# Moving two per-token normalisations of a graph layer from VectorE to ScalarE

## The reference, cut to what matters

```python
def _layernorm(x, axis=-1, eps=1e-05):
    m = jnp.mean(x, axis=axis, keepdims=True)
    v = jnp.var(x, axis=axis, keepdims=True)
    return (x - m) / jnp.sqrt(v + eps)
...
def _L1_gnn_ref(inp, adj, W1, W2, W3):
    h1, h2, h3 = inp @ W1, inp @ W2, inp @ W3          # einsums in the original
    e = leaky_relu(h1 @ h2^T, 0.2); e = where(adj > 0, e, -1e12)
    return relu(softmax(e) @ h3)

def _L1_ffn_ref(x, Wg, bg, W1, b1, W2, b2):
    gate_logits = xf @ Wg + bg
    top_w, top_i = top_k(gate_logits, 2)               # each token goes to 2 of 8 experts
    ...
x = x + _L1_gnn_ref(_layernorm(x), adj, ...)
x = x + _L1_ffn_ref(_layernorm(x), ...)
```

## Time and profile before

| what | us |
|---|---|
| median of 3 runs (lowest, highest) | 1738.74 (1738.03, 1741.6) |
| profiled execution, its own time | 1740.67 |
| its span in the trace | 1738.7 |
| DVE busy in the span | 1017.5 (59%) |
| PE busy in the span | 1287.0 (74%) |
| POOL busy in the span | 812.2 (47%) |
| ACT busy in the span | 740.3 (43%) |

### The profile page before, as it was taken

How to read it: one execution, slowest core, us unless ns; L and a number is a source line. 1 busy time by engine, 2 the same in 40 slices (tenths; PEclk the granted TensorE clock), 3 DMA queues, 4 the chain that set the end, 5 groups by cost and what they waited for, 6 DMA issues and landing times. The chain is left out here.

```text
span 1738.7 us, 34925 instructions
## 1 busy us (share of the span) xinstructions
PE 1287.0 (74%) x8909; PEld 1090.6 (63%) x8909; DVE 1017.5 (59%) x3818; ACT 740.3 (43%) x1710; POOL 812.2 (47%) x839
## 2 busy tenths in 40 slices
PE   3988888837677777349999995767773299999930
PEld 2777666726566667238888884545552189888920
DVE  1788888757767776335555553888885122222236
ACT  2555555515655555214444441443432155555510
POOL 3255555561455554614444443277676144445420
PEclk9999999968989988669999997888876599999975
DMA  6100000000000000145656563122211366766647
GB/s 157 23 1 0 0 0 0 1 1 1 20 28 28 25 25 27 40 133 190 201 189 199 191 201 105 55 71 73 71 36 41 104 214 219 218 217 220 218 133 203
DMA packets 134763, 168.57 MB, mean 97 GB/s; under 512 B 17584, under 2 KB 105520, under 8 KB 134704
## 3 DMA queue, kind: packets, MB, share of 16 engines
q1 hardware_dynamic: 98224, 122.49, 23.6%
q0 software_dynamic: 17408, 35.95, 5.9%
q10 hardware_dynamic: 19072, 9.46, 1.9%
HBM read 123.47 MB, written 44.37 MB: 97 GB/s over the span
## 5 line engine op out<-in xcount | busy, mean ns | idle before, releaser
L1602 POOL DMA_INDIRECT rows<-m_yb,m_dsti x288 | 276.6, 960 | 361.1 <-DVE m_dsti L1734 312.5
L1627 PE MATMUL psum<-m_xT,m_w 128*128 128x256 f32 (+1 forms) x864 | 200.2, 381 | 1.3 <-ACT m_xT L1668 1.3
L964 POOL DMA_INDIRECT dispatch<-a_flat,a1r_pos x128 | 129.9, 1015 | 111.4 <-DVE a1r_pos L945 69.4
L964 POOL DMA_INDIRECT dispatch<-g_flat,g1r_pos x128 | 133.2, 1041 | 74.3 <-DVE g1r_pos L945 37.3
L1627 PEld LDWEIGHTS psum<-m_xT,m_w 128*128 128x128 f32 (+1 forms) x864 | 149.1, 179 | 28.9 <-ACT m_xT L1668 1.9
L1701 DVE TENSOR_TENSOR m_yb<-psum,m_w 128x256 f32<-128x256 f32 x72 | 30.6, 425 | 218.6 <-PE psum L1642 218.6
L1683 ACT ACTIVATE m_sg<-psum,m_w 128x256 f32<-128x256 f32 x288 | 117.9, 471 | 92.4 <-PE psum L1632 91.3
L1632 PE MATMUL psum<-m_xT,m_w 128*128 128x256 f32 x576 | 141.2, 389 | 7.4 <-ACT m_xT L1666 7.4
L1642 PE MATMUL psum<-m_w,m_sg 128*128 128x128 f32 x1152 | 140.5, 275 | 0.6 <-DVE m_yb L1701 0.6
L1676 ACT ACTIVATE m_sg<-psum 128x256 f32<-128x256 f32 (+1 forms) x216 | 78.8, 382 | 142.9 <-PE psum L1627 98.5
L1717 DVE TENSOR_TENSOR m_hT<-psum,m_sg 128x256 f32<-128x256 f32 (+1 forms) x216 | 88.4, 422 | 83.7 <-ACT m_sg L1676 81.1
(11 more groups left out here) (250 smaller groups left out, 2971.2 us busy)
## 6 DMA issues: line engine op xcount, KB each, us to landing
m_w<-in_c_wall SPq DMA_DIRECT2D x72, 578.0 KB, 3.6
m_w<-in_c_wall SPq DMA_DIRECT2D x72, 533.0 KB, 3.4
m_xg<-dispatch SPq DMA_DIRECT2D x144, 130.0 KB, 3.5
g1c_y<-rows SPq DMA_DIRECT2D x32, 256.0 KB
fin_y<-rows ACTq DMA_DIRECT2D x32, 256.0 KB, 3.5
rows<-m_yb,m_dsti POOLq DMA_INDIRECT x288, 3.1
out<-x SPq DMA_DIRECT2D x16, 256.0 KB, 3.0
dispatch<-nobody SPq DMA_DIRECT2D x24, 130.0 KB, 6.8
```

The lines of the kernel that those rows point to most:

```text
L964: pool.indirect_dma_start(out=dest, out_offset=bass.IndirectOffsetOnAxis(ap=self.pos[:, k, p:p + 1], axis=0), in_=flat[:, p, :], in_offset ...
L1602: pool.indirect_dma_start(out=rows_out, out_offset=bass.IndirectOffsetOnAxis(ap=dsti[j][:, t:t + 1], axis=0), in_=yb[j][:, t, :], in_offse ...
L1627: i = pe.matmul(bank[0:cn, TILE * m:TILE * m + TILE], w[j][:, HID * m + c0:HID * m + c0 + cn], xT[j % 2][:, :], start=(m == 0), stop=True, ...
```

## The change

Both normalisations go to ACT, as `x * rs + off` with `off = -mean * rs` (an ACT instruction of the kind Identity, with `rs` as its scale and `off` as its bias, both read from SBUF). DVE forms `off` for the four tiles of a group in one instruction over 128 x 4. That instruction (`head_off`, `flat_off`) needs `rs`, and it stands in DVE's step behind `vector_choose` and ahead of `soft`. On ACT the second normalisation stands ahead of `exp`, the first one between `exp` and `probs_T`. POOL's order is the same, with one more wait in front of each `pow`.

```diff
@@ phase_gnn1
+        ve, rs, off = sb("ve", [128, 2, PG]), sb("rs", [128, 2, PG]), sb("off", [128, 2, PG])
...
             @block.scalar
+                def head_xn(i):
+                    act.wait_ge(*off_ready[0].now(i))
+                    act.wait_ge(*pe_xT.before(i))
+                    act.sem_inc(act_gate.sem, 1)
+                    for p in range(PG):
+                        act.activation(xn[:, p, :], xt(i, p), ACT.Identity, bias=off[:, 0, p:p + 1],
+                                       scale=rs[:, 0, p:p + 1]).then_inc(xn_ready.sem, 1)
+
+                def flat_norm(i, b):
+                    act.wait_ge(*off_ready[1].now(i))
+                    act.wait_ge(*pe_fT.before(i))
+                    R.wait_landed(act, i - 2)
+                    act.sem_inc(act_gate.sem, 1)
+                    for p in range(PG):
+                        act.activation(flat[b][:, p, 0:C], xt(i, p), ACT.Identity, bias=off[:, 1, p:p + 1],
+                                       scale=rs[:, 1, p:p + 1]).then_inc(flat_ready.sem, 1)
...
                 def step(g, b):
                     low(g)
                     head(g + 1)
+                    flat_norm(g - 1, 1 - b)
                     exp(g)
+                    head_xn(g + 2)
                     probs_T(g)
...
-                skewed(act, step)
+                skewed(act, step, first=4)
...
             @block.vector
-                def head_xn(i):
+                def head_off(i):
                     dve.wait_ge(*rs_ready[0].now(i))
-                    dve.wait_ge(*pe_xT.before(i))
-                    for p in range(PG):
-                        dve.tensor_scalar(xn[:, p, :], xt(i, p), mv[:, 0, p, 0:1], rs[:, 0, p:p + 1],
-                                          ALU.subtract, ALU.mult).then_inc(xn_ready.sem, 1)
+                    dve.wait_ge(*xn_ready.before(i))
+                    dve.scalar_tensor_tensor(out=off[:, 0, :], in0=mv[:, 0, :, 0], scalar=-1.0, in1=rs[:, 0, :],
+                                             op0=ALU.mult, op1=ALU.mult).then_inc(off_ready[0].sem, 1)
...
-                def flat_norm(i, b):
+                def flat_off(i):
                     dve.wait_ge(*rs_ready[1].now(i))
-                    dve.wait_ge(*pe_fT.before(i))
-                    R.wait_landed(dve, i - 2)
-                    for p in range(PG):
-                        dve.tensor_scalar(flat[b][:, p, 0:C], xt(i, p), mv[:, 1, p, 0:1], rs[:, 1, p:p + 1],
-                                          ALU.subtract, ALU.mult).then_inc(flat_ready.sem, 1)
+                    dve.wait_ge(*flat_ready.before(i))
+                    dve.scalar_tensor_tensor(out=off[:, 1, :], in0=mv[:, 1, :, 0], scalar=-1.0, in1=rs[:, 1, :],
+                                             op0=ALU.mult, op1=ALU.mult).then_inc(off_ready[1].sem, 1)
...
                 def step(g, b):
                     flat_stats(g - 1)
                     if runs(g - 2):
                         R.vector_choose(dve, g - 2, bR, False)
+                    head_off(g + 2)
+                    flat_off(g - 1)
                     soft(g)
                     if runs(g - 2):
                         R.vector_rows(dve, g - 2, bR)
-                    flat_norm(g - 1, 1 - b)
-                    head_xn(g + 2)
                     head_x(g + 3, 1 - b)
                     norm(g)
                     head_stats(g + 3)
...
             @block.gpsimd
                 def head_rs(i):
                     pool.wait_ge(*vs[0].now(i))
+                    pool.wait_ge(*off_ready[0].before(i))
                     pool.wait_ge(*xn_ready.before(i))
...
                 def flat_rs(i):
                     pool.wait_ge(*vs[1].now(i))
+                    pool.wait_ge(*off_ready[1].before(i))
                     pool.wait_ge(*flat_ready.before(i))
```

More of the change, by code:

```diff
@@ L1801, in phase_gnn1 @@
         st, mv = sb("st", [128, 2, PG, 6]), sb("mv", [128, 2, PG, 2])
-        ve, rs = sb("ve", [128, 2, PG]), sb("rs", [128, 2, PG])
+        ve, rs, off = sb("ve", [128, 2, PG]), sb("rs", [128, 2, PG]), sb("off", [128, 2, PG])
         xn = sb("xn", [128, PG, C])
@@ L1826, in phase_gnn1 @@
         flat_ready = sig("flat_ready", PG)
-        gate = sig("gate")
-        dve_signals = bn + part + vs + [xn_ready, e_steps, rc_ready, x3_ready, flat_ready]\
-            + R.dve_signals + M.dve_signals
+        off_ready = [sig("off0_ready"), sig("off1_ready")]
+        gate, act_gate = sig("gate"), sig("act_gate")
+        dve_signals = bn + part + vs + off_ready + [e_steps, rc_ready, x3_ready] + R.dve_signals + M.dve_signals
         xT_ready, h12_ready, p_ready, pt_ready, fT_ready = sig("xT_ready"), sig("h12_ready", 2), sig("p_ready", 2), sig("pt_ready"), sig("fT_ready")
         low_ready = sig("low_ready", 2)
-        act_signals = [xT_ready, h12_ready, h3_ready, low_ready, p_ready, pt_ready, o_ready, fT_ready] + R.act_signals
+        act_signals = [xn_ready, flat_ready, xT_ready, h12_ready, h3_ready, low_ready, p_ready, pt_ready, o_ready, fT_ready] + R.act_signals
         rs_ready = [sig("rs0_ready"), sig("rs1_ready")]
@@ L1963, in _ @@
             def _(act):
+                def head_xn(i):
+                    if not runs(i):
+                        return
+                    act.wait_ge(*off_ready[0].now(i))
[5 more added lines that the diff above has]
+                def flat_norm(i, b):
+                    if not runs(i):
+                        return
+                    act.wait_ge(*off_ready[1].now(i))
[5 more added lines that the diff above has]
+                                       scale=rs[:, 1, p:p + 1]).then_inc(flat_ready.sem, 1)
                 def head(i):
```

## The result

The changed kernel takes 1768.55 us in the median of 4 runs (1764.85 to 1769.39). The kernel before, on the same chip, takes 1740.17 us (1738.03 to 1743.23). The ratio is 1.0158, with a 95% interval from 1.0135 to 1.018: slower by 28 us. The forecast was 1761 us, in a range of 1752 to 1774.

What follows compares the result with a forecast made beforehand. DVE was taken to bound the loop before, a newly closed loop through POOL's `pow` after. Eleven periods +15.8, tail +5.2 and start +1.5 gave +22.5 us, a median of 1761 us, range 1752 to 1774.

Steps and rivals of the forecast that it cites:

- scatter to `pow`: Loop term on POOL, from a scatter's start to the next `pow`: 10.1 us, with ends 9.99 and 10.78.
- both `pow`: Loop term on POOL, the two `pow` behind a scatter: 2.05 us.
- offset, up to `soft`: Loop term on DVE, both new `off` instructions ahead of `soft`: 0.3 us, from 0.1 to 0.6.
- `soft` to scatter: Loop term from the start of `soft` on DVE to the scatter's start on POOL: 4.31 us, low end 4.14.
- The second DMA: Scatter's second indirect DMA, 1.68 us beside DVE's line 1784 additions; claimed to be held little, near 1.0 us.
- The tail: Last scatter periods behind the eleven: 15.48, 15.48 and 13.0 us, the last period unchanged; +5.2 us in all.
- The start: Layer up to its first scatter: DVE sheds 5.2 us but waits for `pow`; +1.5 us, from -1.8 to +3.
- DVE-PE loop: From `soft` over PE's mix and the reciprocals to the next `soft`: about 16.1 us at PE's low clock.
- POOL loop: Scatter, both `pow`, `off`, `soft`, `vector_rows`, next scatter: claimed to set the period, 16.76 us against 15.32.
- DVE stays the bound: Rival for the loop: DVE still decides, period some 14.5 us, time about 1730, not slower; chance 0.04.
- Shared reads stretch the scatter: Rival: additions hold a scatter DMA and POOL's copies slow DVE's `off`; period 17.5 us, about 1770; chance 0.19.
- The signs named ahead: Expected in the changed profile: DVE idle 0.7 to 2.5 us ahead of the second `off`, scatters 16.8 us apart.

Runs made afterwards that it cites:

- e1b: Kernel before, both normalisations still on DVE, plus one DVE wait for `rs` of group g-1 ahead of `soft`: 1765.91 us, ratio 1.0150.
- e2b: Changed kernel with both offsets behind `vector_rows`; on ACT second normalisation behind `exp`, first at the step's end: 1754.93 us, ratio 1.0074 to the kernel before.
- e10: Kernel before with only `xn` on ACT, between `flat_T` and `mixed_out`, its offset behind `flat_norm` on DVE: 1737.08 us, ratio 0.9996.
- c_after: Changed kernel, unedited, profiled on a chip of the second kind: 1833.54 us, ratio 1.0218 to the kernel before there.

## Why the prediction was right, and where it was too small

**The bound and the mechanism.** Right. Behind the offset stands `soft`, and the loop decides: its four terms are all in the changed trace, and e1b gives a loss of the same size with the wait alone.

| term of the loop | forecast | measured (1200.65 to 1217.53) |
|---|---|---|
| scatter to `pow` | 10.1 | 10.35 |
| both `pow` | 2.05 | 2.04 |
| offset, up to `soft` | 0.3 | 0.23 (0.47 in the group ahead) |
| `soft` to scatter | 4.31 | 4.26 (4.39) |
| sum | 16.76 | 16.88, mean of eleven 16.93 |

The second DMA fell from 1.68 to 1.08 us, as reasoned. What was overlooked is that another one grew: the fifth, at 1205.93, takes 1.26 us for 0.96; these 0.3 us are about what the first term lacks. It starts inside DVE's residual addition, which reads two tiles from SBUF:

```profile
1205.67 0.69 DVE L2114 TENSOR_TENSOR x<-x,g_o 128x512 f32 x1
```

This addition ends at 1206.36 and the DMA at 1207.19, 0.83 us behind it. In eleven periods the error is 17.7 - 15.8 = +1.9 us.

**The tail.** +5.1 us for +5.2. Its parts were 15.48, 15.48 and 13.0 us; measured were 15.23, 15.71 and 12.94. The second is long by a DMA of 1.46 us that starts 0.06 us into the same kind of addition, at 1338.30. That the sum fits to 0.1 us is partly luck, since one part is too short and one too long.

**The start.** This is the mis-sized step: +1.5 us was taken, with +3 as the upper end, and +4.2 came. The forecast set what DVE sheds (up to 5.2 us) against the waits for a `pow` (2.8 us), and gave ACT nothing. e1b shows that the waits alone are +1.1 us. The other 3.0 us came with the move of the work to ACT, what DVE sheds already taken off, and e2b, without the wait, has +3.4. ACT in the changed kernel:

```profile
1097.20 1.63 ACT L1971 ACTIVATE g_xn<-x,g_off,g_rs 128x128 f32<-128x128 f32 x4
...
1102.68 0.60 ACT L1994 ACTIVATE g_h<-psum 128x512 f32<-128x512 f32 x1 [0.26 <-PE psum L1890]
1103.29 1.28 ACT L2030 ACT_TABLE_LOAD   x1
1104.59 0.85 ACT L2030 ACTIVATE g_pr<-g_s 64x256 f32<-64x256 f32 x2
1105.47 1.65 ACT L1971 ACTIVATE g_xn<-x,g_off,g_rs 128x128 f32<-128x128 f32 x4
1107.02 0.57 ACT L2037 ACTIVATE g_pt<-psum 128x512 f32<-128x512 f32 x1
```

and before:

```profile
1098.12 0.60 ACT L1973 ACTIVATE g_h<-psum 128x512 f32<-128x512 f32 x1 [0.26 <-PE psum L1890]
1098.73 1.28 ACT L2009 ACT_TABLE_LOAD   x1
1100.37 0.85 ACT L2009 ACTIVATE g_pr<-g_s 64x256 f32<-64x256 f32 x2 [0.36 <-DVE g_s L2075]
1102.02 0.60 ACT L2016 ACTIVATE g_pt<-psum 128x512 f32<-128x512 f32 x1 [0.79 <-PE psum L1915]
```

Before, the table load of 1.28 us lay in ACT's wait for `g_s`, with 0.36 us to spare. Now ACT comes to it without slack, and the exponential follows it directly. Counted from the layer's first addition (1081.6 and 1083.8), the exponential is at 18.8 us before and at 20.8 now, and `g_pt` at 20.5 and 23.2: the added `g_xn` of 1.65 us between the two gives the last 0.8. From `g_pt` to the first scatter it is 1.4 us more than before, about e1b's 1.2 there.

Not all of the exponential's 2.0 us are ACT's. The first group's matmuls of line 1890 take 1.91 us in the changed kernel and 1.02 before, and ACT waits for them. The granted clock is 0.50 from 1092 to 1097 us (1.2 GHz); before it is 1.00 from 1092.6 to 1098 (2.4 GHz). So 0.9 of the 2.0 us are PE's clock. And a late exponential need not make a late scatter: in e10, with `g_xn` alone on ACT, it comes at 20.8 as well, and the start is only +0.7.

Together loop, tail and start are 27.0 us against the 22.5 of the forecast, and 2.7 of the missing 4.5 are the start's. The medians differ by 28.4 us; the other 1.4 lie outside the layer.

**What hides the rest.** ACT's four two-pointer scalings take 1.65 us, where 1.58 and "a fifth longer" (1.9) were named. The cover was sized wrong, to no harm. The DVE-PE loop was put at 16.1 us, 0.7 below the POOL loop. In the changed kernel DVE idles 1.4 and 1.65 us, in turns, ahead of the two offsets, so the loop without that wait would be some 15.4 us (an estimate: 16.9 less 1.5). The forecast had added up a long group of the old trace (15.72 us, where the mean is 15.32) with a mix of 1.93 us, and the mix now takes 1.52 to 1.64. That e2b measures 16.25 is no proof of the 16.1: its chain runs through ACT's `g_flat`, which its own order puts ahead of PE's transposes and the mix.

**The rivals.** *DVE stays the bound* did not come. *Shared reads stretch the scatter* (17.5 us) did not come in the changed kernel; its 10.78 us term is what e1b shows with the normalisations still on DVE (10.75). By the rule of the Trainium skill that the prediction weighed (page "SBUF — State Buffer", section "Who interferes with whom"), the additions should never stretch a scatter's DMA. e1b again has 1.68 us for a DMA that starts inside them, and the residual addition stretches one too, so the measurement decides against it. Whether the DMA's writing is held or its reading of `g1r_pos` from SBUF, no run separates.

The prediction supposed that it matters where in a batch of additions a DMA starts. That alone is not it. In the loop the 1.68 us DMAs start 0.28 to 0.30 us into their batch, with some 0.85 us to go (e1b's at 1197.28, its batch from 1196.99 to 1198.12). e2b has one at the same place of a batch that takes 0.96 us:

```profile
1179.53 1.14 DVE L1784 SCALAR_TENSOR_TENSOR x<-g1c_y,w,x 128x128 f32 x4 [0.15 <-DVE x L1784]
```

```profile
1179.82 0.96 POOL L964 DMA_INDIRECT dispatch<-g_flat,g1r_pos  x1 [0.30 <-issue]
```

All 1.65 to 1.69 us DMAs stand in the kernels with both normalisations on DVE (the kernel before and the wait alone, on both kinds of chip), eleven in each. Why only there is open.

**The signs named ahead.** DVE idle ahead of the offsets, released by `g_rs`: yes, 1.4 to 1.9 us in the two together, and not before the second alone. POOL's wait near 4.5 us: 4.22 and 4.59. DVE about -30 and ACT about +50 us busy: -27.5 and +52.1. First scatter 1 to 2 us later: wrong, 6.4 us by the time of the span, of which 2.3 lie ahead of the layer.

**One row read short.** DVE's own results cost it more than the 0.15 us that the prediction names: in that group it waits 0.15, 0.15, 0.36 and 0.16 us for them, 0.82 in all. That it waits for no other engine is right, and holds for the whole stretch of the earlier trace rows.

## What to carry to other kernels

Before an instruction is moved forward in an in-order stream, write down what releases it and what stands behind it there: if its releaser stands behind work that its followers release, a loop is closed, and its length is the sum of rows that the old trace already has. Work taken off the busiest engine is worth only what the next loop leaves (here 16.25 us even without the wait, against 15.32 before anything was moved), and a wait that is free at one place of one engine (for a landed buffer, for a table load) can cost in full ahead of a critical instruction on another. Compute the filling of the pipeline apart from its loop: in this case the receiving engine had no slack there.

## What the runs showed of the hardware that was not expected

- Chips differ. The kernel before takes 1740 us on one kind and 1790 to 1796 on two other chips, and the changed kernel is slower by 1.6% on the one and 2.2% on the other. In the traces of the second kind, ACT and DVE often start late behind PE while POOL issues indirect DMAs, in a wait that the profile puts down to "remote": 83.2 us in 11 waits of ACT on line 2021 of the changed kernel, each ended 1.5 to 1.7 us behind the scatter's last DMA. No trace of a chip of the first kind, of six, has a wait marked so. What holds the signal is open; nothing here tested it.
- In attention, too, the profile of c_after puts such waits down to "remote", for DVE's reciprocals on line 1394 (70.8 us in 12), where the changed kernel on the first kind of chip has 56.5 us in 16, released by PE.
- Four ACT scalings of 128 x 128 with both scale and bias from SBUF take 1.65 us: 0.48 us each, started 0.39 us apart.
- An indirect DMA issued on POOL during the residual addition on DVE (TENSOR_TENSOR over 128x512, both inputs in SBUF, 0.69 us) ends 0.83 or 0.84 us behind that addition. In the 14 traces this holds for each of the 96 scatter DMAs of the layer that start 0.05 to 0.56 us into one. They take 0.96 to 1.47 us, where an undisturbed one takes 0.96. Five start at most 0.04 us into one: they take 0.95 to 0.97 us, and most of these additions 0.76 us.
